# Variance of every second tile of the last normalisation by an accumulated row sum and a shifted square on ScalarE

## What is computed

```
def _layernorm(x, axis=-1, eps=1e-05):
    m = jnp.mean(x, axis=axis, keepdims=True)
    v = jnp.var(x, axis=axis, keepdims=True)
    return (x - m) / jnp.sqrt(v + eps)
...
slot_out = jnp.einsum('besh,ehd->besd', h, w2) + b2[None, :, None, :]
out = jnp.einsum('besd,bnes->bnd', slot_out, combine)
...
x = _layernorm(x + _L0_ffn_ref(x, ...), axis=-1)
```

## Time and profile before

| | |
|---|---|
| median of 3 runs | 1914.61 us (1914.0 to 1917.42) |
| the profiled execution | 1911.55 us |
| its span, first to last instruction | 1909.8 us |
| granted TensorE clock, mean | 0.979 |

### The profile page before, as it was taken

How to read it: one execution, slowest core, us unless ns; L and a number is a source line. 1 busy time by engine, 2 the same in 40 slices (tenths; PEclk the granted TensorE clock), 3 DMA queues, 4 the chain that set the end, 5 groups by cost and what they waited for, 6 DMA issues and landing times. The chain is left out here.

```text
span 1909.8 us, 38932 instructions
## 1 busy us (share of the span) xinstructions
PE 1808.9 (95%) x12588; PEld 1287.5 (67%) x12588; DVE 1416.2 (74%) x2902; ACT 1256.9 (66%) x3128; POOL 527.3 (28%) x789
## 2 busy tenths in 40 slices
PE   7899999999999999778999999999999998799988
PEld 5677777878787777555666666666666663588853
DVE  8978888888787879736676767677777776655348
ACT  5646455555555454338889899888989888356514
POOL 1312121213121212341333333333333333100006
PEclk9999999999999999988999999999999999899999
DMA  8113131313131313343344444434343424541166
GB/s 238 54 48 105 46 106 41 112 36 117 35 118 35 119 27 104 127 112 105 101 123 123 123 123 114 133 103 140 103 140 100 141 79 149 151 157 67 67 219 244
DMA packets 126700, 209.25 MB, mean 110 GB/s; under 512 B 26416, under 2 KB 49456, under 8 KB 126256
## 3 DMA queue, kind: packets, MB, share of 16 engines
q1 hardware_dynamic: 112176, 179.21, 30.5%
q0 software_dynamic: 14336, 27.55, 5.7%
HBM read 125.66 MB, written 30.15 MB: 82 GB/s over the span
## 5 line engine op out<-in xcount | busy, mean ns | idle before, releaser
L2037 DVE TENSOR_REDUCE a_mx<-a_shared 128x1 f32<-128x512 f32 x512 | 327.8, 678 | 51.5 <-PE a_shared L2167 50.7
L1974 ACT ACTIVATE a_shared<-a_shared,a_mx 128x512 f32<-128x512 f32 x512 | 341.8, 670 | 23.2 <-DVE a_mx L2037 22.7
L1967 ACT ACTIVATE a_probs<-a_scores 128x512 f32<-128x512 f32 x512 | 300.4, 601 | 55.7 <-PE a_scores L2184 50.6
L2167 PE MATMUL a_shared<-a_ks,a_qs 96*128 96x512 f32 x512 | 209.6, 430 | 14.9 <-ACT a_shared L1974 9.2
L2184 PE MATMUL a_scores<-a_qs,a_ks 98*128 98x512 f32 x512 | 202.0, 406 | 6.3 <-ACT a_probs L1967 5.8
L2139 PE MATMUL a_shared<-link 128*128 128x512 f32 x768 | 199.1, 395 | 2.0 <-DVE a_qk_lo L2024 2.0
L1083 PE MATMUL m_proj<-m_xt_hi,link 128*128 128x512 f32 x448 | 182.3, 407 | 3.8 <-DVE m_acc L777 3.4
L597 ACT ACTIVATE m_xw<-m_added,m_wdt 128x64 f32<-128x64 f32 x256 | 56.0, 329 | 192.7 <-DVE m_xdt L865 192.7
L1084 PE MATMUL m_proj<-m_xt_lo,link 128*128 128x512 f32 x448 | 176.6, 394 | 0.0
L1085 PE MATMUL m_proj<-m_xt_hi,link 128*128 128x512 f32 x448 | 176.3, 394 | 0.0
L777 DVE SCALAR_TENSOR_TENSOR m_acc<-m_proj,m_cw,m_acc 128x511 f32<-128x511 f32 (+2 forms) x216 | 159.3, 747 | 17.6 <-ACT m_acc L536 12.5
(11 more groups left out here) (307 smaller groups left out, 3944.8 us busy)
## 6 DMA issues: line engine op xcount, KB each, us to landing
m_dec<-step_decay SPq DMA_DIRECT2D x64, 256.0 KB, 4.1
a_qs<-link SPq DMA_DIRECT2D x256, 64.0 KB, 2.0
m_ce<-run_decay SPq DMA_DIRECT2D x128, 112.0 KB, 3.1
a_ks<-a_k_hi POOLq DMA_DIRECT2D x192, 64.0 KB, 2.5
e_x<-x SPq DMA_DIRECT2D x11, 1024.0 KB, 5.5
m_xt_in<-x_t_in SPq DMA_DIRECT2D x8, 1024.0 KB, 9.3
m_x_tok<-x_in SPq DMA_DIRECT2D x8, 1024.0 KB, 5.4
x<-m_x_tok SPq DMA_DIRECT2D x32, 256.0 KB, 2.8
```

What stands on the lines that cost most here:

```text
L1967: act.activation(probs[:, n % 2, h, :], scores[t.score_bank(n, h)][:, :], ACT.Exp, scale=-1.0).then_inc(exp_ready, 1)
L1974: act.activation(scored[:, :], scored[:, :], ACT.Exp, scale=-1.0, bias=mx[:, i % 2, h, j:j + 1], accum_out=den[:, i, h, j:j + 1]).then_inc ...
L2037: dve.tensor_reduce(mx[:, i % 2, h, j:j + 1], bank(what)[:, :], AX.X, ALU.min).then_inc(mx_ready, 1)
L2167: pe.matmul(bank(what)[:, :], qs[0:STACK, t.slot(i), h, j * P:(j + 1) * P], ks[0:STACK, t.slot(i), h, :], start=True, stop=True).then_inc( ...
```

## The change

For tiles with even `t` (16 of the 32), DVE no longer runs `bn_stats` and `bn_aggr`; its `scalar_tensor_tensor` also accumulates the row sum. POOL turns the sum into the bias of a square (`shifted`), ACT squares the tile with that bias, scaled so that the accumulated sum is the variance, and writes the squares themselves into a part of `slots_t` that nobody reads. POOL then adds epsilon, takes the power and makes the bias with `tensor_scalar` instructions where `tensor_tensor` stood. Tiles with odd `t` keep the statistics on DVE, with the new POOL instructions. ACT's order is: variance of tile 0; then, for each pair, normalise the even tile, variance of the next even tile, normalise the odd tile. POOL's order is: shift of the even tile, scale and shift of the even tile, scale and shift of the odd tile.

```
@@ gpsimd
+            def scale_and_shift(b, t, mean_factor):
+                n = b * TT + t + 1
+                mean, var, rstd, shift = (mv[:, b, t, 0:1], mv[:, b, t, 1:2],
+                                          norm[:, b, 0, t:t + 1], norm[:, b, 1, t:t + 1])
+                pool.tensor_scalar(var, var, LN_EPS, None, ALU.add).then_inc(rstd_ready, 1)
+                pool.wait_ge(rstd_ready, rstd_had + 2 * n - 1)
+                pool.tensor_tensor(rstd, var, neg_half[:, 0:1], ALU.pow).then_inc(rstd_ready, 1)
+                pool.wait_ge(rstd_ready, rstd_had + 2 * n)
+                pool.tensor_scalar(shift, mean, mean_factor, rstd, ALU.mult, ALU.mult).then_inc(nmr_ready, 1)
+
             for b in range(n_seq):
...
+                for t in range(0, TT, 2):
+                    pair = b * TT // 2 + t // 2 + 1
+                    pool.wait_ge(out_read, read_had + 2 * pair - 1)
+                    pool.tensor_scalar(shifted[:, b, t // 2:t // 2 + 1], mv[:, b, t, 0:1], -SQUARE_SCALE / DM, None,
+                                       ALU.mult).then_inc(shift_ready, 1)
+                    pool.wait_ge(var_ready, var_had + pair)
+                    scale_and_shift(b, t, -1.0 / DM)
+                    pool.wait_ge(mv_ready, mv_had + pair)
+                    scale_and_shift(b, t + 1, -1.0)
@@ scalar
+            def variance(b, t):
+                pair = b * TT // 2 + t // 2
+                act.wait_ge(shift_ready, shift_had + pair + 1)
+                if pair >= TT:
+                    act.wait_ge(var_ready, var_had + pair - TT + 1)
+                act.activation(unused[:, pair % TT, :], residual[b][:, t, :], ACT.Square, scale=SQUARE_SCALE,
+                               bias=shifted[:, b, t // 2:t // 2 + 1], accum_out=mv[:, b, t, 1:2]).then_inc(var_ready, 1)
+
+            variance(0, 0)
             for b in range(n_seq):
...
+                for t in range(0, TT, 2):
+                    normalised(b, t)
+                    if t + 2 < TT:
+                        variance(b, t + 2)
+                    elif b < last:
+                        variance(b + 1, 0)
+                    normalised(b, t + 1)
@@ vector
                     dve.wait_ge(out_done, out_had + n)
+                    if t % 2 == 0:
+                        dve.scalar_tensor_tensor(out=tile, in0=c_bank(b, t), scalar=rc[:, b, t:t + 1], in1=tile,
+                                                 op0=ALU.mult, op1=ALU.add, accum_out=mv[:, b, t, 0:1]
+                                                 ).then_inc(out_read, 1)
+                        continue
```

More of the change, by code:

```diff
@@ L2240, in _ @@
             over_attention(pe, n_seq, step, steps)
+SQUARE_SCALE = 1 / math.sqrt(DM)
 def moe_stage(nc, n_seq, x2, x2_var, front, w1, b1, w2, b2, slot_out, x3):
@@ L2265, in moe_stage @@
         neg_half = sb("neg_half", [P, n_seq * TT])
-        eps_zero = sb("eps_zero", [P, 2])
+        shifted = sb("shifted", [P, n_seq, TT // 2])
         mxd = sb("mxd", [P, 2, ST_TILES])
@@ L2277, in moe_stage @@
         mv = sb("mv", [P, n_seq, TT, 2])
-        norm = sb("norm", [P, n_seq, 4, TT])
+        norm = sb("norm", [P, n_seq, 2, TT])
         lg = work[:, 2048:3072].rearrange("p (t n) -> p t n", t=TT)
@@ L2341, in moe_stage @@
         mv_ready, mv_had = ssb_ready, n_seq
-        var_ready, var_had = dn_ready, n_seq
+        shift_ready, shift_had = dn_ready, n_seq
+        var_ready, var_had = mx_ready, n_seq * ST_TILES
         nmr_ready, nmr_had = mc_ready, n_seq
@@ L2358, in loads @@
             return len(range(p, n_seq, X_BUFS))
+        unused = slots_t[:, 1].rearrange("p e b s -> p (e b s)").rearrange("p (t n) -> p t n", t=TT)
         residual_of = [0, 1, 2, 2, 0, 1, 2, 0]
@@ L2448, in _ @@
             pool.memset(neg_half[:, :], -0.5).then_inc(const, 1)
-            pool.memset(eps_zero[:, 0:1], LN_EPS).then_inc(const, 1)
-            pool.memset(eps_zero[:, 1:2], 0.0).then_inc(const, 1)
-            pool.wait_ge(const, 4)
+            pool.wait_ge(const, 2)
             pool.affine_select(out=ident[:, :], in_=onesf[:, :], compare_op=ALU.is_equal, fill=0.0,
@@ L2458, in _ @@
                 front.row_powers(pool, neg_half[:, 0:TT], b)
-            for b in range(n_seq):
[L2461 to L2472, removed]
+            def scale_and_shift(b, t, mean_factor):
[7 more added lines that the diff above has]
+                pool.tensor_scalar(shift, mean, mean_factor, rstd, ALU.mult, ALU.mult).then_inc(nmr_ready, 1)
+            for b in range(n_seq):
+                for t in range(0, TT, 2):
[7 more added lines that the diff above has]
+                    scale_and_shift(b, t + 1, -1.0)
         @block.scalar
@@ L2539, in _, with normalised @@
                                bias=b1col[:, e:e + 1]).then_inc(h_ready, 1)
-            for b in range(n_seq):
[L2542 to L2545, removed]
+            def normalised(b, t):
+                act.wait_ge(nmr_ready, nmr_had + b * TT + t + 1)
+                act.activation(residual[b][:, t, :], residual[b][:, t, :], ACT.Identity,
+                               bias=norm[:, b, 1, t:t + 1], scale=norm[:, b, 0, t:t + 1]).then_inc(x3_ready, 1)
+            def variance(b, t):
[6 more added lines that the diff above has]
+            variance(0, 0)
+            for b in range(n_seq):
+                for t in range(0, TT, 2):
[5 more added lines that the diff above has]
+                    normalised(b, t + 1)
         @block.vector
@@ L2613, in _ @@
                                       ).then_inc(biased, 1)
-            ln = Chain(dve, ln_v, TT)
+            ln = Chain(dve, ln_v, TT // 2)
             for b in range(n_seq):
@@ L2701, in _ @@
                 if b == 0:
-                    pe.wait_ge(const, 5)
+                    pe.wait_ge(const, 3)
                     transposes(1, range(KT // 2))
```

## The result

| | before | changed |
|---|---|---|
| median of 6 runs | 1914.3 us | 1922.61 us |
| ratio to the kernel before, 95% interval | | 1.0049 [1.0036, 1.0063] |
| span of the profiled execution | 1909.8 us | 1918.8 us |
| start of the last Identity | 1906.56 us | 1915.53 us |

The ratio is 9.4 us of 1914 (7 to 12), the spans differ by 9.0. The prediction said +0.6, with a range that ended at 1920.0.

What follows compares the result with a forecast made beforehand. The prediction took PE's pace to leave DVE 0.6 us to win, and a POOL-ACT loop of 3.20 us a turn to set the end: +0.53 at the last Identity, 0.1 in landing, 1914.61 + 0.6 = 1915.2 us, range 1912.8 to 1920.0.

Steps and rivals of the forecast that it cites:

- PE's pace as the floor: Last 60 us: PE delivers a pair of tiles every 3.43 us, so a faster DVE wins 0.6 us at most.
- DVE's new instruction: On DVE's even tiles, the accumulated sum may add an accumulator read, taken as 0.1 us; a pair then costs 2.4 us.
- The loop between POOL and ACT: POOL's shift releases ACT's square, which releases POOL's scale; the next shift follows both scales: 3.20 us a turn.
- The square's 0.81 us: ACT's square in each turn: 0.52 us to the accumulator read, 0.10 for the bias pointer, 0.19 for the read.
- D: Rival: a table load on ACT before the first square, 1.28 us later, giving 1916.5 us; chance 0.04.
- E: Rival: PE's records hid slack and DVE's saved 13 us show in full, giving 1901.6 us; chance 0.02.
- The square's second wait: From the fifth pair on, ACT's square has a second, already met wait; bounded by 0 and 0.08, taken as 0.04 us.
- the one unknown price: POOL's tensor_scalar, in no row of the trace: bounds 0.10 and 0.29 us, taken as 0.19, five in a turn.
- the 0.14 us from the multiply to the next instruction: On POOL, the gap from each scale's last multiply to the next free instruction, counted twice in a turn.
- the prediction's weight of 80: Five POOL tensor_scalar instructions a turn, 16 turns: 10 ns more on each are 0.8 us at the end.
- C: Rival: POOL's tensor_scalar is dearer than tensor_tensor, 0.25 us each, and the loop decides over 16 turns: 1920.0 us; chance 0.22.
- the predicted 1907.09 for the last Identity: ACT's last Identity starts 3.28 us after the 16th shift at 1903.81, against 1906.56 before: +0.53 us.

## Why the prediction was wrong, point by point

- **PE's pace as the floor**: right. PE's 3.43 us a pair stayed, DVE waits for it in the changed kernel, and the kernel with short statistics shows it alone. Its size, 0.6 us, was read from one execution with PE at the lower clock at the start, and with a hand-over of 0.47 us that measures 0.63. It is 0.4 us in that execution and 2.0 at full clock.
- **DVE's new instruction**: the accumulator read takes 0.08 us, I had 0.10, and it is a record of its own. The Trainium skill says so too ("VectorE: DVE Perf Modes", "Two Vector instructions with no wait between them": an op that also writes out its accumulator is two instructions); the trace agrees. It costs DVE nothing here: where DVE does not wait for PE, a pair of tiles takes (1865.18 - 1856.14) / 4 = 2.26 us (tile 10 and tile 2), where I had 2.4. DVE waits for PE anyway, so this error did not touch the time.
- **The loop between POOL and ACT**: the mechanism was right. It sets the end from the first pair to the last, and moving one instruction out of it removes the whole loss.
- **The square's 0.81 us**: right, 0.82 in the trace; no table load came before it, so D did not happen. E did not either. The square's second wait, for which I added 0.04 us a turn (0.5 in all), costs nothing: the turns are 3.81 us before the fifth pair and after it.
- **The step that failed** is the price of POOL's instructions in the turn, 3.20 us predicted and 3.81 measured. It has two parts. The first is "the one unknown price": "POOL's fixed part hardly depends on the operation, and I take 0.19". The tensor_scalar instructions take 0.217 us (add), 0.236 (shift) and 0.267 (multiply with a pointer operand), over the five of a turn 0.05 more in the mean than taken. By the prediction's weight of 80 that is 4 us at the end, just past the 0.04 us each at which it had said C would show. The second is a term with no doubt attached: the 0.14 us from the multiply to the next instruction, taken over from two tensor_tensor instructions, which measures 0.34, twice a turn. Of these 0.40 us a turn, 0.15 are the multiply's greater length, which the five prices hold; the other 0.25 are the overlap that is gone, 4 us at the end, and no rival had them. The rest of the 0.61 is small: 0.05 on the shift, 0.03 twice on the add, 0.04 twice from power to multiply.
- **With the measured turn the sum closes**: the predicted 1907.09 for the last Identity, plus 16 x 0.61 = 9.8, less 0.5 for the second wait and less 0.7 for the earlier first shift (1854.60 for 1855.33, most of it PE's clock), is 1915.7; measured 1915.53. The kernel with tensor_tensor alone shows the other side: with the assumed prices true, its turn is the predicted 3.20.
- **Rival C** was the case in kind: the loop with dearer instructions. Its price of 0.25 us each, close to the 0.24 measured, gave 1920.0. The upper bound of 0.29 us gave 8.0 us, near what came, but that would have been luck: none of the instructions takes that long, and the lost overlap makes up the difference. A price with no row, weighted 80-fold, asked for a range that reached to its upper bound.

## What to carry to other kernels

Before moving work from a busy engine to two others, draw who waits for whom: where a line of engines becomes a loop, each hand-over and each short instruction in it counts once per turn, and neither engine need look busy (here ACT was at 62% and POOL at 60%). Order the instructions so that the first step of the next item is issued before the last step of this one. And ask first how far the next bound is: here DVE looked like the bound by its busy share and by the chain, and PE stood 0.4 to 2.0 us behind it.

## What was unexpected of the hardware

- On POOL a 128x1 tensor_scalar takes 0.21 to 0.27 us where a tensor_tensor takes 0.19, and two tensor_scalar in a row start 0.34 us apart, two tensor_tensor 0.14. The power, a tensor_tensor, is longer beside them as well: 0.569 us in the mean in the changed kernel, 0.551 in the one with tensor_tensor alone. Why is not shown.
- After an idle time of about 3.6 us PE came back at full clock in one execution of the kernel before and at the lower one in another. It is worth 2.7 us of PE's time here.
